# Linear attention in column tiles: key sums times queries on another engine, an earlier block transpose, an earlier key transpose

## The reference

```python
q = phi(x @ W_Q.T)          # (b, t, 8 heads, 64); phi(u) = elu(u) + 1
k = phi(x @ W_K.T)
v = x @ W_V.T
def step(carry, inp):       # over the 1024 tokens, gamma = sigmoid(decay_log)
    S, z = carry
    qt, kt, vt = inp
    S = g4 * S + einsum('bhi,bhj->bhij', kt, vt)
    z = g3 * z + kt
    num = einsum('bhij,bhi->bhj', S, qt)
    den = sum(z * qt, axis=-1, keepdims=True) + EPS
    return ((S, z), num / den)
gate = sigmoid(x @ W_g_w.T + W_g_b)
y = (outputs * gate) @ W_O.T
```

## Time and profile before

| | |
|---|---|
| median of the runs shown | 2064.12 us (2062.7 to 2065.55) |
| the profiled execution | 2065.1 us, its span 2063.1 us |
| TensorE busy | 1891.8 us, 92% of the span |
| VectorE busy | 1347.6 us, 65% |
| ScalarE busy | 880.6 us, 43% |
| GpSimd busy | 687.2 us, 33% |
| linear-attention stage | about 816 to 1777 us of the span |

### The profile page before, as it was taken

How to read it: one execution, slowest core, us unless ns; L and a number is a source line. 1 busy time by engine, 2 the same in 40 slices (tenths; PEclk the granted TensorE clock), 3 DMA queues, 4 the chain that set the end, 5 groups by cost and what they waited for, 6 DMA issues and landing times.

```text
span 2063.1 us, 36413 instructions
## 1 busy us (share of the span) xinstructions
PE 1891.8 (92%) x12481; PEld 1573.4 (76%) x12481; DVE 1347.6 (65%) x2583; ACT 880.6 (43%) x1717; POOL 687.2 (33%) x622
## 2 busy tenths in 40 slices
PE   8999999999999999788888888888988888899999
PEld 7888888888888888576677667666766666788887
DVE  6566665666688886665555556555656665788885
ACT  6756665566544445233333223333322233244443
POOL 6302222022312222444433443344334434722221
PEclk9999999999999999999999989999999989999999
DMA  7000000000222222100000000000000000223322
GB/s 242 22 1 0 0 0 0 0 0 10 64 41 31 31 31 45 37 9 2 11 11 10 10 10 9 2 10 10 10 10 10 10 5 7 32 56 61 61 61 58
DMA packets 230629, 53.19 MB, mean 26 GB/s; under 512 B 209696, under 2 KB 228768, under 8 KB 230176
## 3 DMA queue, kind: packets, MB, share of 16 engines
q1 hardware_dynamic: 229296, 49.53, 11.9%
q10 hardware_dynamic: 1264, 2.76, 0.4%
HBM read 18.69 MB, written 8.39 MB: 13 GB/s over the span
## 4 chain that ended last, share of the span: by engine, by line
PE 63%; POOL 11%; SPq 9%; issue 7%; DVE 6%; DMA 2%; ACT 2%; ACTq 0%; POOLq 0%; DVEq 0%
PE PS L1203 14%; PE PS L322 11%; SPq L270 9%; PE PS L1212 8%; PE PS L331 7%; PE PS L861 6%; PE PS L832 6%; POOL lin_qsT L1362 3%; PE PS L850 3%; PE PS L1728 2%; PE PS L872 2%; DMA ln_xl<-ln_xn 2%; PE PS L1674 2%; POOL lin_AD L1427 1%; DVE lin_gate L1526 1%
## 5 line engine op out<-in xcount | busy, mean ns | idle before, releaser
L322 PE MATMUL PS<-ln_xh,lin_w 128*128 128x512 f32 x768 | 253.0, 401 | 6.3 <-POOL ln_xl L280 6.3
L1135 ACT ACTIVATE ff_silu<-PS 128x512 f32<-128x512 f32 x192 | 114.4, 597 | 232.8 <-PE PS L1203 204.3
L1170 DVE SCALAR_TENSOR_TENSOR ff_h<-PS,ff_silu 128x512 f32<-128x512 f32 x192 | 131.2, 684 | 107.9 <-PE PS L1203 93.4
L322 PEld LDWEIGHTS PS<-ln_xh,lin_w 128*128 128x128 f32 x768 | 149.2, 194 | 39.8 <-POOL ln_xl L280 4.8
L568 POOL TENSOR_TENSOR qk<-qk,swapped 64x128 f32<-64x128 f32 (+2 forms) x96 | 96.9, 1010 | 239.8 <-DVE swapped L712 234.0
L1154 DVE TENSOR_TENSOR ff_h_lo<-ff_h,ff_h_hi 128x512 fp32r<-128x512 f32 x192 | 164.7, 858 | 0.4
L861 PE MATMUL PS<-probT,v_a 128*128 128x128 f32 x1152 | 153.3, 278 | 0.0
L322 PE MATMUL PS<-ln_xl,lin_w 128*128 128x512 f32 x384 | 153.2, 399 | 0.0
L861 PEld LDWEIGHTS PS<-probT,v_a 128*128 128x128 f32 x1152 | 139.5, 192 | 14.3 <-ACT probT L632 7.4
L832 PE MATMUL PS<-qk 128*128 128x512 f32 (+3 forms) x384 | 145.3, 489 | 1.2 <-POOL qk L568 1.1
L1432 POOL TENSOR_TENSOR lin_yg_lo<-stage,lin_yg_hi 128x512 fp32r<-128x512 f32 x64 | 81.9, 1280 | 180.3 <-ACT lin_yg_hi L1450 179.9
(11 more groups left out here) (190 smaller groups left out, 5587.5 us busy)
## 6 DMA issues: line engine op xcount, KB each, us to landing
ff_raw<-ln_xn SPq DMA_DIRECT2D x464, 32.0 KB, 2.0
ln_xl<-ln_xn SPq DMA_DIRECT2D x288, 32.0 KB, 2.0
out_x<-X SPq DMA_DIRECT2D x15, 512.0 KB, 2.9
X<-in_x SPq DMA_DIRECT2D x7, 1024.0 KB, 5.6
stage<-in_w_lin SPq DMA_DIRECT2D x1, 2048.0 KB, 8.1
stage<-in_w_gate SPq DMA_DIRECT2D x2, 768.0 KB, 7.4
stage<-in_w_up SPq DMA_DIRECT2D x2, 768.0 KB, 8.9
stage<-in_w_down SPq DMA_DIRECT2D x2, 768.0 KB, 10.2
```

The lines of the kernel that those rows point to most:

```text
L322: last = nc.tensor.matmul(out, w, x, start=n == 0, stop=n == len(terms) - 1)
L1170: nc.vector.scalar_tensor_tensor(h[:, f % 2, :], PS[:, NB_GU + f % NB_GU, :], W_SCALE, silu[:, f % NB_GU, :], ALU.mult, ALU.mult).then_inc ...
```

## The change

1. `sums_by_query` moves from GpSimd to VectorE. There it waits for the scan (`z_done`), copies the last column in first halves (`tensor_copy`, then a wait for it), and multiplies `z[j]` by the query features. GpSimd's query scalings no longer wait for the scans, but for the query features alone.
2. The order on VectorE changes with it: behind feature item 3 the scan of tile 0, behind 4 its product, behind 5 the scan of tile 1, behind 6 its product, behind item 7 the scans of tiles 2 and 3 and then their products. Before, the scan of tile 0 stood behind item 3 and the other three behind item 7.
3. `dve_blocks` stands directly behind `dve_normalise`, ahead of the loop over chunks; before it stood behind the masked scores of the second chunk and `gate_scale`.
4. On TensorE the fourth chunk's keys come at the end of the third chunk's turn; before they came behind the fourth chunk's `outputs`, just ahead of the `state` that needs them.

```diff
@@ LinearSignals
     def pool_open(self, pool):
-        open_signals(pool, self.qs_done, self.yg_lo_done, self.s_decayed, self.zq_done,
-                     self.z_kept)
+        open_signals(pool, self.qs_done, self.yg_lo_done, self.s_decayed)
     def dve_open(self, dve):
         open_signals(dve, self.phi_done, self.ks_done, self.ad_done, self.den_done, self.inv_done, self.z_done,
+                     self.z_kept, self.zq_done,
                      self.scale_done, self.s_done, self.yg_done, self.x_done)
@@ GpSimd, turn
                     for j in range(NP):
-                        pool.wait_ge(z_done.sem, z_done.at(b, NP * half + j + 1))
+                        pool.wait_ge(phi_done.sem, phi_done.at(b, 2 * NP * half + 2 * j + 1))
                         nc.gpsimd.tensor_tensor(qsT[:, j, :]..., qT[:, j, :]..., Gq[:, j, :]..., ALU.mult)
-                        sums_by_query(b, half, j)
-            def sums_by_query(b, half, j):
-
-                if half == 0:
-                    nc.gpsimd.tensor_scalar(z_last[:, j:j + 1], z[j][:, UN - 1:UN], 1.0, None, ALU.mult).then_inc(z_kept.sem, 1)
-                    pool.wait_ge(z_kept.sem, z_kept.at(b, j + 1))
-                nc.gpsimd.tensor_tensor(z[j], z[j], qT[:, j, :], ALU.mult).then_inc(zq_done.sem, 1)
@@ VectorE
+            def sums_by_query(b, half, j):
+
+                dve.wait_ge(z_done.sem, z_done.at(b, NP * half + j + 1))
+                if half == 0:
+                    nc.vector.tensor_copy(z_last[:, j:j + 1], z[j][:, UN - 1:UN]).then_inc(z_kept.sem, 1)
+                    dve.wait_ge(z_kept.sem, z_kept.at(b, j + 1))
+                nc.vector.tensor_tensor(z[j], z[j], qT[:, j, :], ALU.mult).then_inc(zq_done.sem, 1)
@@ VectorE, turn
                     for it in range(2 * NP):
                         phi_item(b, half, it)
-                        if it == 2 * NP - 1:
-                            for j in range(1, NP):
+                        if it in (3, 5):
+                            key_sums(b, half, it // 2 - 1)
+                        elif it in (4, 6):
+                            sums_by_query(b, half, it // 2 - 2)
+                        elif it == 2 * NP - 1:
+                            for j in range(NP // 2, NP):
                                 key_sums(b, half, j)
-                        elif it == 3:
-                            key_sums(b, half, 0)
+                            for j in range(NP // 2, NP):
+                                sums_by_query(b, half, j)
...
                     inverse(b, half)
                     nln.dve_normalise(dve, nturn)
+                    nfront.dve_blocks(dve, nturn, (front, b * NHALF + half))
                     for c in range(UT):
...
                         if c == 0:
                             gate_scale(b, half)
-                            nfront.dve_blocks(dve, nturn, (front, b * NHALF + half))
@@ TensorE, turn
                         outputs(b, half, c)
-                        if c == UT - 1 and ch + 1 < NC:
-                            keys(b, half, c)
                         if ch + 1 < NC:
                             state(b, half, c)
                         if c >= 2:
                             out_projection(b, ch - 2)
-                        if c + 2 < UT:
+                        if c + 1 < UT and ch + 2 < NC:
                             keys(b, half, c + 1)
```

## The result

| | before | after |
|---|---|---|
| median | 2064.12 us | 1887.69 us (1887.54 to 1887.85) |
| ratio | | 0.9145, 95% interval 0.9106 to 0.9185 |
| span of the profiled execution | 2063.1 us | 1886.0 us |
| mean granted clock | 0.962 | 0.999 |
| TensorE busy | 1891.8 us, 92% | 1843.9 us, 98% |

The change took 176 us, 8.6%, from the time.

A forecast was written before the change was run, and what follows sets the result against it. Beside TensorE's own work, GpSimd ahead of the denominators and the moves' landing ahead of the last projection bound each half. Savings of 4.9 + 2.6 + 3.2 = 10.7 us over 15 halves, plus 14, gave 1889 us; range 1866 to 1940.

The forecast's parts named there:

- The sum: Whole kernel: 10.7 us saved in each of 15 halves, 161, plus 14 at the edges, giving 1889 us.
- Products late by 0.9 us a half: Ahead of the denominators: products 1.2 us late in first halves, 0.6 in second; mean 0.9 instead of 5.83, saving 4.9.
- my 1.4 us: VectorE ahead of the denominators: delay charged for contention with four GpSimd query scalings, bounds 0 and 4 x 1.0 us.
- The first half: Edge term: the very first half's 10.2 us wait shrinks to about 0.7, less 2.0 for masking the decay table.
- rival B: VectorE and GpSimd obstruct each other at the products, 3.5 to 4 us late, clock partly low: 1935 us, chance 0.16.
- The signs: Named as showing it wrong: products over 1.2 us, scans 2 us or more, scalings 2.2 us, projections over 19.5 us.
- The clock: Denominators and values at full clock: 6.5 us against 9.1, saving 2.6 us a half, bounds 0 and 2.6.
- with a wait that short the clock should not fall: Step for denominators and values: with the wait ahead cut to about 0.9 us, TensorE's granted clock stays up.
- The chunks: With the transpose earlier, the chunks take about 20.2 us instead of 23.45, saving 3.2 us a half.
- the 0.3 us charged for the late transpose: In the chunks: charge because the second chunk's masked scores on VectorE come 1.1 us late behind the transpose.
- 21.27 x 0.94: In the chunks: TensorE's own work in a first half, put at 20.0 us.
- The keys: Fourth keys sooner removes a 0.8 us scaled-keys wait once a batch; worth nothing while the moves' landing is late.

The follow-up runs named there:

- the doubled scan: The kernel after with the scan of tile 3 done twice in each half, values unchanged: 1911.11 us, ratio 0.9256.
- products alone: The kernel before with only the key-sum products moved to VectorE in the new order and query scalings released by the features: 1961.34 us, ratio 0.9494.
- transpose and keys: The kernel before with the block transpose directly behind the normalisation and the fourth keys a slot sooner, products still on GpSimd: 2000.83 us, ratio 0.9684.
- keys alone: The kernel before with only the fourth chunk's keys moved to the end of the third chunk's turn: 2066.63 us, ratio 1.001.
- products and keys: The kernel before with products on VectorE and fourth keys sooner, block transpose left late: 1960.37 us, ratio 0.9486.

## Why the prediction was right, point by point

**The sum.** 1889 us predicted, 1887.69 measured. The mechanism was right, but that the two agree to 1 us is partly luck, since the terms were off in both directions. By the spans, 177.1 us were saved: 15 halves of 59.84 less 48.77, 166.1 us; the start up to the first half's denominators 5.6 (844.00 to 838.37); what lies behind the last half's denominators 5.4 (321.5 to 316.1). Predicted were 161 and 14. Within a half, by the table of means in the experiments, the way from scores to denominators gave 5.4 (4.9 predicted), denominators and values 1.8 (2.6), the chunks 3.7 (3.2) and the projections 0.2 (nothing).

**Products late by 0.9 us a half.** A first half's denominators start 22.2 us in, and a second half's 21.6 (1131.56 less 1109.34; 1179.37 less 1157.76), 0.9 and 0.3 us later than they could; I had 1.2 and 0.6. The unit costs were right: a product 0.69 us alone, a copy 0.14, and the doubled scan shows that each microsecond in this queue counts. Of the four scalings, one product (1.82) is held in a first half and one of the early scans in a second (up to 2.36, median 1.87, in the rows of the scan by source line); my 1.4 us were somewhat too many.

**The first half** is the largest single miss: its wait is 3.44 us where I had 0.7. There GpSimd's scalings wait for the decay tables and start only at 830.38, ahead of the last scans and beside them and the products. The timeline of VectorE in that half:

```profile
831.45 3.54 DVE L1504 TENSOR_TENSOR_SCAN lin_AD<-lin_tmp_a,lin_kT 128x512 f32<-128x512 f32 x2
834.92 0.12 DVE L1511 COPY lin_z_last<-lin_AD 128x1 f32<-128x1 f32 x1
835.07 1.52 DVE L1513 TENSOR_TENSOR lin_AD<-lin_AD,lin_qT 128x512 f32<-128x512 f32 x1
836.52 0.14 DVE L1511 COPY lin_z_last<-lin_AD 128x1 f32<-128x1 f32 x1
836.69 1.57 DVE L1513 TENSOR_TENSOR lin_AD<-lin_AD,lin_qT 128x512 f32<-128x512 f32 x1
```

and GpSimd's in the same half, four scalings in a row until 837.7:

```profile
830.38 7.34 POOL L1362 TENSOR_TENSOR lin_qsT<-lin_qT,lin_decay_q 128x512 f32<-128x512 f32 x4 [9.65 <-ACT lin_decay_q L1433]
```

This is rival B: 3 us late, and 8.25 us at a granted clock of 0.79 for the denominators and values behind it. It comes back once, in the last batch's first half: there one scan takes 2.35 us and two products 1.82 each, TensorE waits 0.7 and 1.2 us for late feature items, and the projections take 22.1 us instead of the 20.0 of the batches before:

```profile
1497.20:1519.32 22.12, 20.22 (x97) 16.08 (x97) 16.59 (x23) 12.41 (x21) 7.67 (x6) 1.00 0.00 1
```

In the other 14 halves one instruction is held for about 1.1 us. That it is the release of the scalings by the features alone which keeps the rest out of the way fits these timelines, but no run has the products on VectorE with the old release. The Trainium skill's exclusive lock ("SBUF — State Buffer", "Who interferes with whom") agrees with the holds of 1.1 us for a GpSimd operation that started 0.02 us earlier; its caution in "Perfetto Trace Analysis", "Optimizing Scalar/DVE Operations", that moving work between these engines might not help, was not borne out here: the same product took 1.26 us or more on GpSimd, with TensorE waiting, and takes 0.69 alone on VectorE.

**The signs.** Four of the signs that I had named for being wrong are there, though the forecast came out: products of over 1.2 us (1.82, in every first half but the first, which has 1.52 and 1.57), scans of 2 us or more in 10 of the 16 halves, query scalings of 2.3 us in six, and projections of 20.0 us ahead of nearly every first half's denominators. They were badly chosen. The halves with a single hold have their products only 0.9 and 0.3 us late; it is the number of holds in one half that counts.

**The clock.** 6.66 us measured for the stretch of denominators and values, 6.5 predicted. The saving was over-sized all the same, 2.6 us where 1.8 were there, because the batch that I had cut has two of the slower halves (9.50 and 8.71, mean of all 8.61). And the products alone show that this term isn't tied to its own wait, as the step "with a wait that short the clock should not fall" had it: that stretch did reach 1.00, but the chunks and projections fell from 0.98 and 0.97 to 0.93 and 0.95, since other idle stayed. Products alone gave 104 us, transpose and keys 65, all three 176 to 178: 7 to 9 us are there only together (the intervals of the ratios leave this open by some 6 us; the table of means, 11.1 us a half less 6.5 and 4.1, has 7 as well).

**The chunks.** 20.26 and 19.54 us against my 20.2 for both. SyncE starts its moves 2.0 us in (1140.24; 2.2 predicted), they land 13.8 us in (13.95). In a second half the low part of the moved tokens ends the wait, as worked out. In a first half the 0.3 us charged for the late transpose didn't appear, and 21.27 x 0.94 gave too much for TensorE's own work: the mean clock of a stretch that holds idle time too is no exact measure of how much longer its matmuls took.

**The keys.** "Worth nothing while the landing is late, because the next wait takes it up" was shown with the landing late twice (keys alone; products and keys). Its size once free, 8 to 10 us, was under-estimated at 6.

## What to carry to other kernels

Work moved from one engine to another is priced by the queue it joins, instruction by instruction, and by what the old engine still has to do: here GpSimd kept four instructions, and where they start decides whether they hold the other engine for a microsecond each. A small edit can be worth nothing until the wait behind it is gone, so look at which wait ends last before and after each one. Idle time of TensorE cost a second time in clock here, and the whole of that was only won with both long waits gone; what is left in nearly every half is under 0.8 us at a time, at a clock of 1.00. And take the size of a stretch from all its repetitions: two of them, cut from one batch, over-sized the clock's term by 0.8 us a half.

## What the runs showed of the hardware

- Taking one of two regular waits away gave the stretch behind it the full clock (0.76 to 1.00) and lowered it elsewhere: with the products alone the chunks went from 0.98 to 0.93 and the projections from 0.97 to 0.95. The mean clock of the whole execution is 0.962 before, 0.978 with the products alone, 0.968 with transpose and keys, 0.999 with all three parts.
- Behind waits of 1.6 to 1.8 us ahead of the denominators (the scan done twice) the granted clock stayed at 1.00 in every half but the first (a wait of 4.70 us, then 0.69). Behind the 3.44 us of the first half it was 0.79 in the kernel after, and behind the same wait 1.00 with the products alone.
- A GpSimd scaling and VectorE's product behind the same feature item start 0.02 us apart, and the order decides: the scaling was first and the product was held (1.82 us instead of 0.69). Four short statistics in other places (0.4 us each) changed how many such holds there are, and cost 9 to 11 us in all.
